# Cross-attention, two layers: the first layer's context norm in one operation per tile, its weight at the exits from PSUM, its shift in the biases, and another order of loads

## The reference, cut to what matters

```python
qn  = layer_norm(q_feat)  * g_q  + be_q         # over 256
kvn = layer_norm(kv_feat) * g_kv + be_kv        # over 192
q = qn  @ Wq.T + bq
k = kvn @ Wk.T + bk
v = kvn @ Wv.T + bv
x = q_feat + softmax(q @ k.T) @ v @ Wd.T + bd   # layer 0
...                                             # layer 1, eight heads on the raw context, then a norm
```

## Time and profile before

| | |
|---|---|
| median of 3 runs | 511.05 us |
| the profiled execution | 510.73 us, span 508.9 us |
| PE busy | 475.9 us, 94% of the span |
| DVE / ACT / POOL busy | 333.3 / 291.6 / 244.1 us |
| chain that ended last | PE 72%, DVE 10%, DMA 7%, ACT 5% |

### The profile page before, as it was taken

The page is one execution under the profiler, slowest core; times in us unless marked ns, Lnnn a source line. Parts: engine busy times, 40 slices in busy tenths (PEclk is TensorE's granted clock), DMA queues, the critical chain, the costliest instruction groups (busy, mean ns, idle before and its releaser), DMA issues.

```text
span 508.9 us, 7590 instructions
## 1 busy us (share of the span) xinstructions
PE 475.9 (94%) x2424; PEld 394.5 (78%) x2424; DVE 333.3 (65%) x681; ACT 291.6 (57%) x480; POOL 244.1 (48%) x151
## 2 busy tenths in 40 slices
PE   0989999999979999999999999999999999999992
PEld 0877787777868888888888888888888888788891
DVE  5999866566565658565756585667656765755467
ACT  4667377466565656666556565666556564656222
POOL 4636664455845353637271727263635453353004
PEclk9999999999999999999999999999999999999997
DMA  8413013757756576465656474747484745561002
GB/s 265 137 44 124 1 47 106 235 163 236 229 168 217 176 205 206 166 207 165 206 165 225 146 222 150 243 140 246 141 254 142 236 150 181 167 204 43 0 2 82
DMA packets 53974, 81.97 MB, mean 161 GB/s; under 512 B 5792, under 2 KB 43072, under 8 KB 53824
## 3 DMA queue, kind: packets, MB, share of 16 engines
q1 hardware_dynamic: 44992, 50.16, 34.3%
q10 hardware_dynamic: 8960, 31.54, 16.5%
HBM read 49.16 MB, written 32.51 MB: 160 GB/s over the span
## 4 chain that ended last, share of the span: by engine, by line
PE 72%; DVE 10%; DMA 7%; ACT 5%; issue 2%; POOL 1%; SPq 1%; DVEq 0%; ACTq 0%; POOLq 0%
PE ps_scores L611 25%; PE ps_o L634 6%; PE ps_o L635 5%; PE ps_o L638 5%; PE ps_o L637 5%; PE ps_o L636 5%; DMA probs_t_lo<-scratch 3%; DMA scratch<-probs 3%; PE ps_task L561 2%; PE ps_task L560 2%; PE ps_task L559 2%; PE ps_out L559 2%; DMA ctx_raw<-in_context 2%; ACT probs L975 1%; PE ps_out L561 1%
## 5 line engine op out<-in xcount | busy, mean ns | idle before, releaser
L506 POOL TENSOR_TENSOR probs_t_lo<-probs_t_lo,probs_t_hi 128x1024 fp32r<-128x1024 f32 (+1 forms) x75 | 146.2, 1960 | 180.6 <-ACT probs_t_hi L987 180.4
L987 ACT ACTIVATE probs_t_hi<-probs_t_lo 128x1024 fp32r<-128x1024 f32 (+1 forms) x75 | 64.6, 881 | 44.3 <-DMA probs_t_lo<-scratch 44.2
L634 PE MATMUL ps_o<-probs_t_hi,val_hi 128*128 128x512 f32 (+1 forms) x144 | 56.6, 393 | 2.8 <-DVE o_lo L1356 2.6
L1301 DVE RECIPROCAL row_inv<-row_sum 128x1 f32<-128x1 f32 x72 | 11.4, 160 | 70.6 <-PE ps_scores L611 68.6
L635 PE MATMUL ps_o<-probs_t_lo,val_hi 128*128 128x512 f32 (+1 forms) x144 | 56.6, 393 | 0.0
L638 PE MATMUL ps_o<-probs_t_lo,val_rem 128*128 128x512 f32 (+1 forms) x144 | 56.4, 391 | 0.0
L637 PE MATMUL ps_o<-probs_t_hi,val_rem 128*128 128x512 f32 (+1 forms) x144 | 56.0, 389 | 0.0
L636 PE MATMUL ps_o<-probs_t_hi,val_lo 128*128 128x512 f32 (+1 forms) x144 | 55.9, 388 | 0.0
L1338 DVE STREAM_TRANSPOSE probs<-probs 128x1024 f32<-128x1024 f32 x30 | 37.4, 1245 | 24.8 <-ACT probs L975 24.8
L611 PE MATMUL ps_scores<-key_hi,q_hi 128*128 128x512 f32 x144 | 46.6, 405 | 2.2 <-DVE neg_scores L1314 1.7
L1338 DVE STREAM_TRANSPOSE neg_scores<-neg_scores 128x1024 f32<-128x1024 f32 x30 | 37.2, 1242 | 14.4 <-ACT neg_scores L975 14.4
(11 more groups left out here) (247 smaller groups left out, 1090.3 us busy)
## 6 DMA issues: line engine op xcount, KB each, us to landing
probs_t_lo<-scratch SPq DMA_DIRECT2D x240, 128.0 KB, 3.0
scratch<-neg_scores ACTq DMA_DIRECT2D x30, 512.0 KB, 3.3
scratch<-probs ACTq DMA_DIRECT2D x30, 512.0 KB, 3.8
ring<-in_weights_a SPq DMA_DIRECT2D x9, 512.0 KB, 5.2
ring<-in_weights_b SPq DMA_DIRECT2D x9, 512.0 KB, 6.0
ring<-in_keys_t SPq DMA_DIRECT2D x4, 512.0 KB, 3.4
ctx_raw<-in_context SPq DMA_DIRECT2D x2, 768.0 KB, 9.1
ring<-in_context SPq DMA_DIRECT2D x16, 96.0 KB, 2.7
```

Of the source, the lines that this page charges most:

```text
L506: nc.gpsimd.tensor_tensor(pt_lo[b][:, t, k, :], pt_lo[b][:, t, k, :].bitcast(f32), moved_part(j, k).bitcast(f32), ALU.subtract).then_inc(m ...
L634: pe.matmul(o0, val_hi[b][:, kt, :], hi, start=first, stop=False)
L987: act.activation(moved_part(j, k), pt_lo[b][:, t, k, :].bitcast(f32), ACT.Copy)\
```

## The change: what it does

- The context is normed by one operation per tile, without weight and shift: tiles 0 to 3 by DVE as (row - mean) * rstd, tiles 4 to 7 by ACT as rstd * row + (-mean * rstd), for which DVE makes the four negated means (`shift_means`). Centring, scaling on ACT and DVE and POOL's addition fall away for both batches. POOL's power runs in two halves.
- The weight g_kv comes as two columns of 128 (`gains`) and is applied where products leave PSUM: in the rounding and splitting of the turned context (`round_chunk`, `split_chunk`) and of B (`round_b`, `split_b0`).
- The shift be_kv goes into the biases: `fold_bias` on DVE multiplies a weight row with be_kv and sums it, twice per side, and adds bk or bv; ACT spreads the result (`spread_bias`), and T_VEC and T_OUTB use it. So T_VEC moves on PE from ahead of x's transposes and behind A to behind all transposes of batch 0, right ahead of the queries. The second side's fold stands on DVE between the rounding of the queries and `sum_shift(0)`.
- Loads: the context of batch 0 in two halves with the first weights between; q_rows on ACT's queue, first; only one of kv_rows' two rows; three small transfers for the gains.

```diff
+            sp.dma_start(ctx_raw[:, 0:CTX_HALF, :], ...).then_inc(ctx_loaded[0], 16)
             sp.dma_start(ring[0][:, :], weights_a[0]).then_inc(ring_loaded[0], 16)
+            sp.dma_start(ctx_raw[:, CTX_HALF:KT, :], ...).then_inc(ctx_loaded[1], 16)
+            sp.dma_start(kv_rows[:, :], rows_kv[1].partition_broadcast(P)).then_inc(kv_rows_loaded, 16)
...
-                rsqrt(b, 0, KT, 2 * b + 2)
-                pool.wait_ge(kv_rows_loaded, 16)
-                bias_tiles(b, range(CTX_HALF, KT), done + QT, ctx_normed[1])
+                rsqrt(b, 0, CTX_HALF, 3 * b + 2)
+                rsqrt(b, CTX_HALF, KT, 3 * b + 3)
...
+            act.dma_start(q_rows[:, :, :], rows_q.partition_broadcast(P)).then_inc(q_rows_loaded, 16)
+            act.dma_start(ident[:, :], identity).then_inc(ident_loaded, 16)
             act.dma_start(cols[:, :], vectors).then_inc(cols_loaded, 16)
+            gain(gains[:, 0:1], 0)
+            gain(gains[0:REM, 1:2], P)
+            gain(gains[REM:P, 1:2], P)
...
+            def norm_context(b):                                     # ACT
+                act.wait_ge(means_made, b + 1)
+                for t in range(CTX_HALF, KT):
+                    n = b * LN_TILES + t
+                    act.activation(kvn[b][:, t, 0:CTX], ctx_raw[:, b * KT + t, :], ACT.Identity,
+                                   scale=rstd[:, n:n + 1], bias=neg_means[:, n:n + 1]).then_inc(ctx_normed[1], 1)
+            def spread_bias(n):
+                act.wait_ge(bias_folded, n // DT + 1)
+                act.activation(spread[:, n, :], ones[:, :], ACT.Copy, scale=bias_cols[:, n:n + 1])\
+                    .then_inc(spread_made, 1)
...
+            def norm_context(b):                                     # DVE
+                dve.wait_ge(rstd_made, 3 * b + 2)
+                for t in range(CTX_HALF):
+                    n = b * LN_TILES + t
+                    dve.tensor_scalar(kvn[b][:, t, 0:CTX], ctx_raw[:, b * KT + t, :], moments[:, n, 0:1],
+                                      rstd[:, n:n + 1], ALU.subtract, ALU.mult).then_inc(ctx_normed[0], 1)
+            def fold_bias(side, raw, loaded):
+                dve.wait_ge(loaded, 16)
+                for k in range(DT):
...
+                    dve.tensor_tensor_reduce(
+                        out=probs[:, n * CTX:(n + 1) * CTX], in0=raw[:, first:first + CTX], in1=kv_rows[:, :], scale=1.0, scalar=0.0,
+                        op0=ALU.mult, op1=ALU.add, accum_out=bias_parts[:, n:n + 1]).then_inc(bias_summed, 1)
...
+                dve.tensor_tensor(bias_cols[:, n], bias_parts[:, n],
+                                  cols[:, C_BK + side * DT:C_BK + (side + 1) * DT], ALU.add).then_inc(bias_folded, 1)
...
+                    dve.scalar_tensor_tensor(key_lo[b][:, n], src[:, 0:BANK], gains[:, 0:1],
+                                             key_hi[b][:, n].bitcast(f32), ALU.mult, ALU.subtract)\
                         .then_inc(chunk_split, 1)
...
             split_queries(T_Q0b, 0, 1, 0)
+            fold_bias(1, ring[1], ring_loaded[1])
             sum_shift(0, range(QT))
```

More of the change, by code:

```diff
@@ L756, in free @@
                     pe.wait_ge(task_free, task - 1)
-            pe.wait_ge(spread_made, DT)
-            pe.wait_ge(ring_loaded[0], 16)
-            raw = ring[0]
-            for k in range(DT):
-                pe.matmul(vec_bank[:, DIM:2 * DIM], spread[:, k, :], raw[:, k * DIM:(k + 1) * DIM],
-                          start=(k == 0), stop=(k == DT - 1))
             pe.wait_ge(ident_loaded, 16)
@@ L770, in _ @@
             absorb(T_A0b, 1)
+            for c in range(X_CHUNKS, CHUNKS):
+                turn_chunk(0, c)
+            pe.wait_ge(spread_made, DT)
+            pe.wait_ge(cols_loaded, 16)
+            raw = ring[0]
+            for k in range(DT):
+                pe.matmul(vec_bank[:, DIM:2 * DIM], spread[:, k, :], raw[:, k * DIM:(k + 1) * DIM],
+                          start=(k == 0), stop=(k == DT - 1))
             for n in range(3):
@@ L776, in _ @@
             last.then_inc(task_done, 1)
[L777 to L778 removed]
             pe.wait_ge(chunk_split, X_CHUNKS)
[L780 removed]
+            pe.wait_ge(task_free, T_A0b + 1)
             queries(T_Q0, 0, 0)
@@ L1124, in _ @@
             act.wait_ge(ones_set, 1)
-            act.wait_ge(cols_loaded, 16)
-            for n in range(2 * DT):
-                act.activation(spread[:, n, :], ones[:, :], ACT.Copy, scale=cols[:, C_BK + n:C_BK + n + 1])\
-                    .then_inc(spread_made, 1)
+            act.activation(row_sum[:, 0:1], ones[:, 0:1], ACT.Copy)
             scale_tiles(0, range(KT, LN_TILES), 1)
@@ L1144, in _ @@
             round_queries(T_Q0b, 0, 1, 0)
+            for n in range(DT, 2 * DT):
+                spread_bias(n)
             exp(-1, 0)
@@ L1422, in ln_moments @@
             def ln_moments(b, first, end):
-                done = b * LN_TILES + (QT if first == 0 else 0)
+                done = b * LN_TILES + (QT + first if first < KT else 0)
                 for i, t in enumerate(range(first, end)):
@@ L1435, in ln_centre @@
                 for t in tiles:
-                    n = b * LN_TILES + t
-                    if t < KT:
-                        dst, src, gain = kvn[b][:, t, 0:CTX], ctx_raw[:, b * KT + t, :], kv_rows[:, 0, :]
-                    else:
-                        x_tile = b * QT + t - KT
-                        dst, src, gain = xn[:, x_tile, :], resid[:, x_tile, :], q_rows[:, 0, :]
-                    dve.scalar_tensor_tensor(dst, src, moments[:, n, 0:1], gain, ALU.subtract, ALU.mult)\
-                        .then_inc(centred, 1)
@@ L1514, in _ @@
             split_a(T_A0b, 1, -1.0)
+            dve.wait_ge(kv_rows_loaded, 16)
+            dve.wait_ge(cols_loaded, 16)
+            fold_bias(0, ring[0], ring_loaded[0])
+            dve.wait_ge(gains_loaded, 48)
+            for c in range(2, CHUNKS):
+                split_chunk(0, c)
             dve.wait_ge(task_done, T_VEC + 1)
@@ L1517, in _ @@
             dve.tensor_scalar(neg_w_row[:, :], vec_bank[:, DIM:2 * DIM], -1.0, None, ALU.mult).then_inc(task_free, 1)
-            for c in range(2, CHUNKS):
-                split_chunk(0, c)
             dve.wait_ge(task_free, T_VEC + 1)
```

129 lines of the change are left out of this document (74 added, 55 removed).

## The result

The changed kernel took 515.77 us (median of 9 runs, 513.89 to 517.28), the kernel before 511.43 in the same rounds (9 runs): a ratio of 1.0073, 95% interval 1.0049 to 1.0098, which is 2.5 to 5.0 us slower. The profiled execution took 515.24 us (span 513.4), 4.5 more than the one shown of before. Slower was forecast, by 1.8 us; the time lies outside the range.

The account below looks back on a forecast made before the run. Bound: waits from loads through DVE and POOL to PE's queries, then PE, busy 94%. 1.6 + 0.9 - 0.7 = +1.8 on 510.73 gives 512.5, forecast as 512.8 for a median; range 510.7 to 514.7 us.

Parts of the forecast that it names:

- the first of the walk: Transfers at the start: x and q_rows share both queues, adding 0.7 us, so x lands at 5.1.
- the upper end of 6.91: Upper bound for x's landing, in us: where x and q_rows together had landed in the kernel before.
- x behind all of q_rows: Rival, start: the two transfers share so badly that x lands at 6.9; 1.8 us added, 514.6; chance 0.08.
- vector products: PE before the queries: four row-vector products 0.87 us and twelve narrow ones 1.25, together 2.1, queries at 22.4.
- The conflict at the port that the forecast charged to w_lo: DVE's w_lo beside POOL's additions to x: 0.3 us, bounds 0 to 0.7.
- the forecast's 1.6: Start of the queries on PE: 22.4 us instead of 20.8, so 1.6 us later.
- The second fold: DVE between the queries' rounding and the first minimum, where PE waits: +0.9 us.
- -0.7, bounds 0 and -0.7: Batch 1: 0.25 us of PE's idle time and 0.45 of slack up to the scores come back.
- 0.1 us each on ACT: Per-row factors on the roundings: 0.1 us each on ACT, in batch 1 beside PE's products.
- The rule that I set aside: Batch 0, DVE's first-half norms beside POOL's power: by the rule the means come some 0.6 us later; nothing was taken.
- the slower clock: Rival, PE before the queries at its lower clock: vectors 1.0 us more, queries up to 2.9; 515 to 516; chance 0.08.
- the microsecond that I named as refuting me: Sign: the forecast is wrong if the stretch of 98 to 150 us changes its length by more than a microsecond.

Follow-up runs that it names:

- e12: e7 plus an unread load of 256 KB of plain rows, first on ACT's queue beside x; one execution, no ratio; x landed at 5.83 us.
- e13: Changed kernel with the identity moved behind the column vectors and gains on ACT's queue, q_rows still first there; ratio 1.0053 to the kernel before.
- e1: Changed kernel with q_rows moved back to SyncE's queue, second, behind x; ratio 1.0044 to the kernel before.
- e7: e1 with the identity also moved behind the column vectors and gains on ACT's queue; ratio 1.0027 to the kernel before.
- e6: Changed kernel with the second fold made behind the first score minimum, its spread moved along; ratio 1.0080 to the kernel before.
- e5: Changed kernel with batch 1's negated means ahead of DVE's tiles and POOL's residual adds behind batch 1's shift; ratio 1.0054 to the kernel before.
- e3: Kernel before with only q_rows moved, from second on SyncE's queue to first on ACT's; ratio 1.0056 to the kernel before.
- e9: e7 with the first fold and its spread ahead of rounding A, vector products between the halves of the context's transposes; ratio 0.9997 to the kernel before.
- e11: e7 with batch 1's negated means made first and POOL's residual adds behind batch 1's shift; ratio 1.0012 to the kernel before.
- e10: Changed kernel with the edits of e9, e11 and e6 together; ratio 0.9985 to the kernel before.
- e2: Changed kernel with the three gains transfers issued behind the mask, last on ACT's queue; ratio 1.0101 to the kernel before.

## Why the prediction was wrong

The step that failed is the first of the walk: "I take both queues sharing from the start: 262 KB at the 360 GB/s of a full stretch is 0.7 us, so x at 5.1". x landed at 7.32, past the upper end of 6.91. The rate came from a stretch of plain rows; the row that showed this transfer almost by itself was in the earlier trace rows, from x's landing at 4.38 to 6.91, 2.5 us, and the rival "x behind all of q_rows" read it so. That rival came, with 0.4 us more than it priced. By the rule in the Trainium skill, "DMA: Bandwidth & Descriptors", section "Queues, rings and completion order", x shares with the other queue packet by packet; e12 and e13 agree with it, about one for one, but the price is not in the bytes: a copied packet held an engine for 0.19 us and a plain one for 0.08, and part of the delay is engines that stood idle, which the walk had no term for.

Behind that landing the walk held, term by term (us):

| step | forecast | kernel after |
|---|---|---|
| x landing to end of w_lo | 7.4 | 7.10 (7.32 to 14.42) |
| w_lo to the negated means | 2.95 | 2.91 (to 17.33) |
| ACT's four tiles | 1.9 | 1.85 (17.61 to 19.46) |
| doubling, A, a_lo | 1.35 | 1.37 (to 20.83) |
| first fold | 0.9 | 0.74 (to 21.57) |
| spread | 0.7 | 0.69 |
| vector products | 2.1 | 2.22 (22.36 to 24.58) |
| queries, from x's landing | 17.3 | 17.26 |

That the sum is right to 0.04 us is partly luck: single terms are off by up to 0.3. And the path between is not the one walked. ACT's tiles began 0.28 us behind the means, because ACT was still rounding x's second chunk (17.12 to 17.72 in the chain). x was late there because of one of POOL's four additions (shortest, median and longest in ns; first and last start):

```profile
L438 POOL TENSOR_TENSOR xn<-xn,q_rows x4: 726/730/1782, 11.2 to 13.2; 128x256 f32<-128x256 f32 x4
```

The last one began with DVE's w_lo (13.19) and took 1.78 us for 0.73. The conflict at the port that the forecast charged to w_lo (0.3 us) fell on POOL here; in e1, where w_lo began during the last addition, it fell on w_lo (1.64 us for 1.23). In e7, where w_lo starts behind the additions, the longest took 0.90 and ACT waited for the means, as in the walk.

So the queries' +3.76 is the forecast's 1.6 and the 2.2 by which x was mis-sized. e7, where x lands at 4.28, measures +1.33 there, for a walk whose own x was at 5.1 and whose weights, at 9.90 in e7, landed as forecast (9.9).

The second fold was forecast at +0.9: the distance grew by 0.77 from the queries to the second score block. By e6 this is work that DVE has to do on either side of the first minimum.

The second wrong step is batch 1's, "-0.7, bounds 0 and -0.7". From the values to the scores it cost 0.47 more (12.72 us for 12.25): the 0.25 of idle time came back and with it 0.17 more (7.07 for 7.49 up to the transposes), but behind them 0.89 were lost. The forecast argued that DVE and POOL lose work there and that TensorE bounds the stretch. Of the 0.89, 0.26 are the key splits, which now carry the weight (four from start to end 3.11 us, 61.13 to 64.24, against 2.85): the forecast priced the factor on ACT alone ("0.1 us each on ACT") and laid it beside TensorE's products. The other 0.64 is their start, 2.49 us behind the transposes' for 1.85. In the kernel before, DVE's scalings lost time (2.96 us for 1.40 in batch 0), but then POOL's residual adds gave way, one of them taking 2.22 us for 0.74, and DVE's shift products ran at full pace (POOL and DVE of before, from their timelines):

```profile
52.27 7.32 POOL L492 TENSOR_TENSOR resid<-resid,rem_sum 128x256 f32<-128x256 f32 x8
```

```profile
51.18 2.96 DVE L1451 SCALAR_TENSOR_TENSOR kvn<-kvn,rstd,kv_rows 128x192 f32<-128x192 f32 x4
54.07 0.41 DVE L1479 CUSTOM_DVE_ANT_0 ctx_raw<-xn,rem_sum 128x256 f32<-128x256 f32 x1
54.41 0.41 DVE L1479 CUSTOM_DVE_ANT_0 ctx_raw<-xn,rem_sum 128x256 f32<-128x256 f32 x1
```

After, the same eight adds took 5.66 and DVE gave way:

```profile
53.96 5.66 POOL L496 TENSOR_TENSOR resid<-resid,rem_sum 128x256 f32<-128x256 f32 x8
```

e5 shows the collision; why one or the other gives way is open. The rule that I set aside in "SBUF — State Buffer", section "Who interferes with whom", of the Trainium skill, says that DVE in its two-port mode and GpSimd shut each other out: in batch 1 the trace agrees (2.61 us beside the adds, 1.24 in e5 without them); beside POOL's powers in batch 0 the same four tiles took 1.25.

Of the other rivals, the slower clock cost little. x's eight transposes stand on the chain at half pace (0.20 us apart from 15.14 to 16.73), but the means were made at 17.33, so this can have cost at most the 0.28 us named above. A's products ran 0.21 us apart, against 0.12 before, but ended at 19.44 while ACT was at its tiles until 19.46; the vector products and the queries ran at full pace. The stretch from head 0's query products to its values was 36.06 us for 37.00, under the microsecond that I named as refuting me. In the other runs it was 34.9 to 37.7, e3's 37.7 with an unchanged program there among them, and it ends on spilled probabilities that return by DMA. What it gives back in one execution (0.94 here) is not put down to the change.

The sum, then: +1.8 forecast, +2.2 from x and +1.2 from batch 1 make 5.2, against 5.33 at the batch-1 scores; at the end the ratio gives +3.7 (2.5 to 5.0). A single execution can't follow the loss that far: from the batch-1 scores to the end of the span the profiles took 446.5 us (e9) to 451.8 (e3), 449.9 before and 449.1 after. That e7 and e11, which undo the one and then the other, are at +1.4 and +0.6 agrees in size with both, though their intervals overlap; shown by the times are e3's loss and that e9 and e10 are faster than the changed kernel.

## What to carry to other kernels

Price a transfer beside the one that the kernel waits for from a row where it runs by itself, or by moving it and reading the landing, not by its bytes: issued together with x, 64 KB of identity cost x 1.24 us, 256 KB of plain rows 1.55 and 256 KB of one copied row 3.15. The first transfer on the chain wants the queues to itself at its start; the identity, issued behind the column vectors, cost it nothing. When a change takes work off an engine, look at what then runs beside its neighbour on a shared port: a wait that keeps the two apart (1.0 us from transposes to scores in e5 and e11) can be worth more than the work that was saved (0.42 up to the transposes).

## What the hardware showed that was not expected

- Copies of one 2 KB row moved at under half the rate per engine time of plain rows (0.18 MB in 59% of 2 us, 0.22 MB in 31%), and 128 of them delayed the other queue's transfer by 3.15 us instead of 1.55.
- Three transfers of 4-byte rows kept ACT's queue at issuing for 3.15 us (2.31 to 5.46) in the kernel after, and 1.72 in e7; put last, they left x's landing as late as it was (7.56, e2).
- One POOL addition that began with DVE's w_lo took 1.78 us for 0.73, and one that ran beside DVE's four shift products 2.22 for 0.74, while w_lo (1.23) and the products (0.41) lost nothing. In e1 w_lo began during an addition and took 1.64, and the four additions lost nothing (2.78).
- The first products after an idle start ran at half pace although the granted clock reads 1.00 there: A's twelve took 2.7 us (16.73 to 19.44). The row for 8 to 20 us of the kernel after (busy time of PE, PEld, DVE, ACT, POOL; clock, DMA share, GB/s):

```profile
8.00:20.00 12.00, 4.86 (x23) 4.89 (x24) 9.76 (x38) 6.13 (x14) 6.94 (x7) 1.00 0.69 244
```
